# Last attention: the output product with blocks of Wo as the standing operand, copied and turned back

## What is computed

```
def _L1_xattn_ref(x, memories, ln_g, ln_b, Wq, Wkv, Wm, Wo, bo):
    xn = (x - mu) * rsqrt(var + EPS) * ln_g + ln_b
    q = _split_heads(xn @ Wq)                      # 16 heads of 64
    k, v = halves of xn @ Wkv                      # 100 own keys
    mem = _split_heads(memories @ Wm)              # 722 memory keys, also values
    k = concatenate([k, mem]); v = concatenate([v, mem])
    attn = softmax(q k^T / 8)
    out = attn v -> (b, n, 1024)
    return out @ Wo + bo                           # (b, n, 1024) @ (1024, 512)
x = x + _L1_xattn_ref(...)
```

## Time and profile before

| | us |
|---|---|
| runs shown | 1721.60, 1725.01, 2905.01 |
| median | 1725.01 |
| profiled execution | 1737.0 |
| its span, first to last instruction | 1735.3 |
| PE busy in the span | 1599.8 (92%) |
| DVE busy | 1135.9 (65%) |
| ACT busy | 822.8 (47%) |
| mean granted TensorE clock, of full speed | 0.957 |

### The profile page before, as it was taken

The page is one execution under the profiler, slowest core; times in us unless marked ns, Lnnn a source line. Parts: engine busy times, 40 slices in busy tenths (PEclk is TensorE's granted clock), DMA queues, the critical chain, the costliest instruction groups (busy, mean ns, idle before and its releaser), DMA issues.

```text
span 1735.3 us, 32814 instructions
## 1 busy us (share of the span) xinstructions
PE 1599.8 (92%) x12252; PEld 1407.2 (81%) x12252; DVE 1135.9 (65%) x2075; ACT 822.8 (47%) x1543; POOL 252.5 (15%) x293
## 2 busy tenths in 40 slices
PE   6999599999999689989999999999999759999992
PEld 5787499999999589779888888988888649999991
DVE  3687667777777452257676766767676557766774
ACT  2344255555555432256465555546454424444442
POOL 1112201010110030021111111111101032112212
PEclk9999699999999889999999999999999779999996
DMA  6997266666666444230111101120203036656653
GB/s 191 353 393 247 60 246 207 212 220 206 218 206 216 141 141 178 86 114 20 53 42 33 54 24 51 28 59 20 59 19 98 16 114 214 221 197 203 228 199 88
DMA packets 93531, 246.06 MB, mean 142 GB/s; under 512 B 32582, under 2 KB 39238, under 8 KB 78326
## 3 DMA queue, kind: packets, MB, share of 16 engines
q1 hardware_dynamic: 84214, 223.15, 38.0%
q0 software_dynamic: 9216, 21.53, 5.6%
HBM read 179.14 MB, written 65.50 MB: 141 GB/s over the span
## 4 chain that ended last, share of the span: by engine, by line
PE 49%; DVE 4%; DMA 1%; ACT 1%; issue 1%; POOL 0%; DVEq 0%; POOLq 0%; SPq 0%; ACTq 0%
PE banks L2011 14%; PE banks L1164 10%; PE banks L2072 5%; PE banks L1141 5%; PE banks L2056 4%; PE banks L2045 4%; PE banks L2088 3%; PE banks L2032 3%; DMA token_sums<-e_y,e_dest 1%; PE banks L1133 1%; ACT a_P L2327 0%; DVE a_nmax L2194 0%; DVE a_cl L2172 0%; DVE e_lo L1217 0%; ACT a_ch L2306 0%
## 5 line engine op out<-in xcount | busy, mean ns | idle before, releaser
L2011 PE MATMUL banks<-a_ch,a_wm 128*128 128x362 f32 (+1 forms) x1024 | 285.0, 340 | 6.1 <-DVE a_cl L2172 6.1
L1217 DVE TENSOR_TENSOR e_lo<-e_raw,e_hi 128x2048 fp32r<-128x2048 f32 x97 | 224.3, 2312 | 53.2 <-ACT e_hi L1301 50.6
L1164 PE MATMUL banks<-e_xh,e_hi 128*128 128x256 f32 x768 | 216.7, 282 | 0.5 <-DVE e_hf L1246 0.5
L1164 PE MATMUL banks<-e_xl,e_hi 128*128 128x256 f32 x768 | 216.1, 281 | 0.0
L1164 PE MATMUL banks<-e_xh,e_lo 128*128 128x256 f32 x768 | 215.8, 281 | 0.0
L1301 ACT CAST e_hi<-e_raw 128x2048 fp32r<-128x2048 f32 x98 | 185.9, 1905 | 13.4 <-PE banks L1141 13.4
L2011 PEld LDWEIGHTS banks<-a_ch,a_wm 128*128 128x128 f32 x1024 | 186.1, 190 | 7.0 <-DVE a_cl L2172 6.6
L2011 PE MATMUL banks<-a_cl,a_wm 128*128 128x362 f32 (+1 forms) x512 | 168.9, 330 | 0.0
L1112 POOL DMA_INDIRECT token_sums<-e_y,e_dest x32 | 77.3, 2414 | 578.8 <-DVE e_y L1274 315.3
L1141 PE MATMUL banks<-e_hi,e_hh 128*128 128x512 f32 x384 | 152.6, 397 | 0.0
L1164 PEld LDWEIGHTS banks<-e_xh,e_hi 128*128 128x128 f32 x768 | 145.2, 189 | 8.7 <-DVE e_lo L1217 3.1
(11 more groups left out here) (294 smaller groups left out, 3363.5 us busy)
## 6 DMA issues: line engine op xcount, KB each, us to landing
e_raw<-wout SPq DMA_DIRECT2D x50, 1024.0 KB, 6.2
e_raw<-w SPq DMA_DIRECT2D x34, 1024.0 KB, 21.8
slot_rows<-a_zero SPq DMA_DIRECT2D x66, 514.0 KB, 11.5
e_raw<-wgate SPq DMA_DIRECT2D x17, 1024.0 KB, 4.9
e_raw<-wup SPq DMA_DIRECT2D x17, 1024.0 KB, 5.0
a_craw<-ctxT SPq DMA_DIRECT2D x32, 361.0 KB
e_xs<-slot_rows SPq DMA_DIRECT2D x9, 514.0 KB, 6.7
a_craw<-slot_rows SPq DMA_DIRECT2D x9, 514.0 KB
```

The costliest lines, as they stand in the source:

```text
L1164: mm = nc.tensor.matmul(ps[:, bank, 0:CAP], w[:, cc, cut], x[:, cc, :], start=t == 0, stop=t == len(terms) - 1)
L1217: nc.vector.tensor_tensor(lo[g % 2][i], raw[q % RAW][:], hi[g % 2][i].bitcast(F32), ALU.subtract)\
L2011: mm = nc.tensor.matmul(ps[:, 6 + half, 0:wide], w[:, cc, cut], x[:, cc, start:start + wide], start=cc == 0 and t == 0, stop=cc == DC - 1 ...
```

## The change

The output product keeps blocks of Wo (128 x 128) as the standing operand and moves the 100 attended columns: for each of 4 blocks of 128 output features, 8 products are accumulated into 100 columns of bank 7, so that the output lies with its features in the partitions. ACT copies the 128 x 400 result into rxT (a new function `output_copied`), and one step later PE turns it back with 4 transposes against the identity (`output_back`), into the same bank and the same shape as before. The addition moves to that step (BACK_AT = 2). Statistics, rows, turn, logits and copy move one step later; rank stays at 7. The splits stay in m=2 to 5.

```diff
@@ -1821,7 +1821,7 @@
-    OUTPUT_AT, STATS_AT, ROWS_AT, TURN_AT, LOGITS_AT, COPY_AT, RANK_AT = 1, 2, 3, 4, 5, 6, 7
+    OUTPUT_AT, BACK_AT, STATS_AT, ROWS_AT, TURN_AT, LOGITS_AT, COPY_AT, RANK_AT = 1, 2, 3, 4, 5, 6, 7, 7
     SPLIT_AT = {2 + cc: cc for cc in range(DC)}
@@ -1863,6 +1863,7 @@
+        oc, ocs = k.sem("a1_output_columns"), k.sem("a1_output_copied")
@@ -2084,9 +2085,17 @@
                     pe.wait_ge(ys, IC * (b + 1))
                     keys_copied(b + 1, OUTPUT_AT)
-                    for j in range(IC):
-                        mm = nc.tensor.matmul(ps[0:T, 7, :], yT[:, j, :], s1.wo[:, j, :],
-                                              start=j == 0, stop=j == IC - 1)
+                    for cc in range(DC):
+                        for j in range(IC):
+                            mm = nc.tensor.matmul(ps[:, 7, T * cc:T * cc + T], s1.wo[:, j, 128 * cc:128 * cc + 128],
+                                                  yT[:, j, :], start=j == 0, stop=j == IC - 1)
+                    mm.then_inc(oc, 1)
+
+                def output_back(b):
+                    pe.wait_ge(ocs, b + 1)
+                    keys_copied(b + 1, BACK_AT)
+                    for cc in range(DC):
+                        mm = nc.tensor.transpose(ps[0:T, 7, 128 * cc:128 * cc + 128], rxT[:, cc, :], k.ident[:])
                     mm.then_inc(od, 1)
@@ -2129,6 +2138,8 @@
                     if m == OUTPUT_AT + 1:
+                        after(pe, ocs, b)
+                    if m == BACK_AT + 1:
                         after(pe, os_, b)
@@ -2143,6 +2154,8 @@
                     if prev:
                         attended(p - 1, *back(b, m))
+                    if m == BACK_AT and b >= 1:
+                        output_back(b - 1)
@@ -2161,6 +2174,7 @@
                 output(B - 1)
+                output_back(B - 1)
                 route_turn(B - 1)
@@ -2269,7 +2283,7 @@
-                    if m == OUTPUT_AT and b >= 1:
+                    if m == BACK_AT and b >= 1:
                         add_output(b - 1)
@@ -2345,6 +2359,10 @@
+                def output_copied(b):
+                    act.wait_ge(oc, b + 1)
+                    nc.scalar.copy(rxT[:].rearrange("p c t -> p (c t)"), ps[:, 7, 0:DC * T]).then_inc(ocs, 1)
@@ -2379,6 +2397,8 @@
                     if exists(p - 1):
                         attended(p - 1, (m - 1) % IC)
+                    if m == OUTPUT_AT and b >= 1:
+                        output_copied(b - 1)
@@ -2399,6 +2419,7 @@
                 expert_weights_high(1)
+                output_copied(B - 1)
                 rows_copied(B - 1)
```

## The result

The changed kernel takes 1733.36 us (median of 10 runs, 1727.94 to 1735.79) against 1724.51 before (10 runs). The ratio is 1.0053 with a 95% interval of 1.0041 to 1.0065, so it is slower by 7 to 11 us, most likely 9. The one run of 2905.01 us among those of before has no part in the ratio, which is taken from the fast runs alone. The forecast was 1730, which is 5 more than before, and the median lies in its range of 1716 to 1745. That range takes in rival 2 (1716) and rival 3 (1739) as well, and 1733.4 lies between the forecast and rival 3, so the time alone does not say which account holds.

The account below looks back on a forecast made before the run. PE bounds the last attention stage, so each PE microsecond counts. Six batches +3.3, the seventh +0.8 and the stage's end +1.5 sum to +5.6, say +5, on the 1725.0 us median: 1730, range 1716 to 1745.

Parts of the forecast that it names:

- rival 2: Output product: weight loads hide entirely, 86 ns a pass, group 5.6 us, kernel 1716 us; chance 0.11.
- rival 3: Routing steps: gap behind route_best stays 1.15 us in m=7 and m=3 costs 1.3, kernel 1739 us; chance 0.15.
- What bounds the kernel: Last attention stage: PE runs without a gap through plain steps, so every PE microsecond counts; late maxima hold it up.
- The allowance of 2.66 us: Each attention step: the maximum may start 2.66 us after its scores before PE is held up.
- The product: Turned output product: 64 passes at 0.112 us, the larger of load and columns; group 7.3 us, +0.2 a batch.
- Rival 1: Output product: loads and matmuls serialise, group 12.6 us, kernel 1772 us, +2.7%; chance 0.05.
- Turning back: Four PE transposes of the copied output, with their ends: +0.61 us a batch.
- The steps: Moved addition and routing steps: a new stall of +0.8 us in m=3, and -1.05 us behind route_best.
- the new stall: In m=3: the addition, moved to m=2 behind a split, makes the maximum late, +0.8 us a batch.
- the gap: PE's 1.15 us delay in m=6 behind route_best; moving route_best off a split saves 1.05.
- The seventh batch and the last steps: Batch without a split: +0.8 us; moving route_best between its last two steps 0, between -2 and +2.
- The end of the stage: After the last batch nothing covers the chain: product +0.2 and +0.2, copy 0.57, transposes 0.6; +1.5 us.

Follow-up runs that it names:

- e5: Changed kernel with each 128-column block of Wo cut into pairs of 64 in the two column halves: 1725.29 us, 0.9962 of the kernel before.
- e1: Kernel before with only the routing steps moved, old output product and addition kept: 1720.33 us, 0.9963 of the kernel before.
- e3: Changed kernel with the first split moved from m=2 to m=1, ahead of no addition: 1726.81 us, 1.0015 of the kernel before.
- e6: Changed kernel with the last batch's output product in its old form, no copy or turning back there: 1737.29 us, 1.0037 of the kernel before.
- e8: Changed kernel with only 75 of the 100 attended columns moved in the output product: 1748.19 us, one run.
- e4: Changed kernel with only 50 of the 100 attended columns moved in the output product: 1761.59 us, one run.
- e7: Changed kernel with pairs of 64, turned back and added in m=1, last product old, logits 6, earlier routing steps as before: 1720.67 us, 0.9938 of before.
- e9: Kernel with pairs of 64 standing columns, with only 50 of the 100 attended columns moved: 1714.69 us, one run.

## Why the prediction was right

**What bounds the kernel** held: in the stage every PE microsecond and every late maximum showed at full size. The allowance of 2.66 us was right to 0.1 where it was tried: 3.39 gave a stall of 0.82 by the distances (0.73 by the rule), 2.16 gave none.

**The product**: 7.3 us forecast, 7.3 to 7.4 measured (distance +0.28, forecast +0.2). A pass costs the larger of load and columns: 112 ns, as forecast. (Where the prediction reads "8.7 ns a column" for a load it must be 0.87, 87 ns for 100 columns; its 0.11 us for 128 is right.) Rival 1, load and columns one after the other at 196 ns, is out, and with it, for fp32 blocks over all 128 rows, the rule of the Trainium skill that the prediction weighed ("TensorE: Matmul & The Clock Gate", packing small matmuls). Rival 2, hidden loads at 86 ns, is out for blocks of 128 columns, and its 86 ns is the price of a pair of 64 (e5).

**Turning back**: +0.61 forecast, +0.59 measured.

**The steps**: the new stall +0.8, measured +0.82; the gap -1.05, measured -1.10 and +0.09 left, so -1.01. Rival 3, two gaps for one, is out by both distances, and e1 and e3 show each cause by itself. A batch with a split came to +0.67 for +0.55.

**The seventh batch and the last steps**: forecast +0.8, and the distances from m=0 to m=6 of batch 7 add up to 70.85 against 71.01, so -0.16. I had put moving route_best between the last two steps at 0 between -2 and +2; here it gave about -1. That is luck of this profile: in e6 and e8, where nothing up to there sets them apart from the change, the sum is 71.7, +0.7, which is close to the forecast.

**The end of the stage** is the term of the sum that was mis-sized: "+1.5", measured +3.5. Copy and transposes were right (0.49 and 0.64). The product there was put at +0.2 and again +0.2 "as the first 1.3 us ran below full clock". It took 2.25 more than the old one (10.00 against 7.75), because the low clock lasted 5.5 us of it and not 1.3: at half clock a pass takes 213 ns instead of 112, so about half of those 5.5 us is lost (2.6), and 7.3 + 2.6 is the 10.0 measured. I had carried the low stretch of the old product over to the turned one. That the form of the product is what keeps the clock low longer is borne out by the runs above, each a single execution, and why it does so is not shown. Part of the 3.5 is luck of the profile of before: over all profiles of either form (7.77, 8.59, 8.36, 8.51 against 11.26, 10.96, 11.36) the difference is 2.9.

The sum was +5.6; with the measured terms it is 6 x 0.67 - 0.16 + 3.5 = 7.4, which is the stage's 667.8 - 660.4. The medians say +9 (7 to 11). The up to 2 us between them are no more than what the last steps vary by (10.30 or 11.17, 17.52 or 18.43 us, above), and the stages ahead vary too; no run tells which it was. The forecast of +5 was low, by 2 at the end of the stage and 0.7 in the batches; in the profile the seventh batch, 1 below its forecast, made up for part of it.

## What to carry to other kernels

Turning a product round so that fewer columns move pays only if the pass doesn't then wait for its weights: here 100 moving fp32 columns take 86 ns and a load of 128 standing ones 112, so the turned product did fewer column steps and took longer, until the blocks were cut into pairs of 64 in the two column halves. Read the distance between two unhindered loads and between two passes before choosing. And a chain of small work costs by what stands before it in its queue: how late the first instruction after it may start was one number in this stage (2.66 us), and each placement could be weighed against it by hand.

## What the runs showed that I had not expected

- The clock of TensorE can fall in the midst of back-to-back passes. With 50 moving columns in passes of 112 ns it went from 2.4 to 1.2 GHz in six of seven products, 3.9 to 5.4 us after their start, and the kernel took about 27 us more than the change, which does more work. With 75 and with 100 columns it held in all seven places inside the stage. The busy share does not show the difference: PE and PEld were busy in all of the first 4.0 us both with 50 and with 100 columns.
- How soon the clock came back in the last product went with its form as well: 1.3 to 2.9 us after its start in the old form, 4.9 to 5.7 in the turned form, not at all with 75 or 50 columns. These are one execution each.
- Untouched stages differ by up to 15 us between two profiled executions (the first scores of the last attention start at 756.70 in before and at 741.84 in e3), more than the whole effect. Most of it goes with the group of runs: 741.84 to 743.87 in e1 to e4, 746.79 to 751.07 in e5 to e7, 753.75 and 754.14 in e8 and e9. The kernel before itself took 1725.39, 1731.86 and 1733.03 us beside these three groups.
